# Set-up order of a DLRM tower: look-ups among the first folds, additions after the products, gathers in step with set-up

## Chip, cores and metric

The kernel runs on one core of one Trainium2 chip. The time is device microseconds of the whole program, as the median of its runs. PE is TensorE, DVE VectorE, ACT ScalarE, POOL GpSimd, SP SyncE. All arithmetic is in float32.

## What is computed

26 embedding tables are looked up for 512 rows of ids (EMB 32); a compressed interaction network of two layers without an activation between is summed over the embedding axis, and three dense layers follow:

```python
e  = stack([tbl_f[ids[:, f]] for f in range(26)], axis=1)         # 512 x 26 x 32
x1 = einsum('bik,bjk,hij->bhk', e, e, W1) + b1[None, :, None]      # H = 128
x2 = einsum('bik,bjk,hij->bhk', x1, e, W2) + b2[None, :, None]
z  = concatenate([x1, x2], axis=1).sum(-1)                         # 512 x 256
h  = maximum(concatenate([z, dense_ctx], axis=1) @ W_top1 + b_top1, 0)
h  = maximum(h @ W_top2 + b_top2, 0)
y  = h @ W_top3
```

## The kernel before

The batch is four tiles of 128 rows. Per tile there are four kinds of work.

**Rows.** Ten small tables stay in SBUF (`small`). `one_hot(t)` (L644) makes one-hot matrices of their ids on DVE; `look_up(t, pick)` (L301) multiplies them on PE with the tables, in eight picks that alternate between banks 7 and 6; `pick(t, i)` (L671) masks and sums the result on DVE into `rows`. A look-up waits for the mask of the pick two before it. The other 16 fields come by gathers of POOL, one indirect DMA each, in three parts (`PARTS`: fields 0 to 12, 13 to 22, 23 to 25; of them gathered 5 to 12, 18 to 22 and 23 to 25). In tile 0 the gathers wait for `s_sf`, the count of ACT's set-up copies, by `PACE`; in the later tiles POOL waits for landings at the five places in `PAUSES`.

**Products.** `turn(t, part)` (L692) transposes rows into `prod` on DVE. `take_factor` (ACT, L556) copies a part as factors into bank 6 or 7; `spread` (ACT, L547) writes its block-diagonal form `diag`. `half_a` and `half_b` (DVE, L701, L705) form the products of pairs of fields. `step(t, s)` (L350) then does tile t's product matmuls in four steps of 8 + 8 (L367, L375); ACT's `evict` (L519) copies them to `t0` and `t1`, in tile 0 also the bands, four copies a step, counted by `s_eg`.

**Dense part.** `z2`, `z2_low`, `z1`, `layer1`, `layer2`, `layer3` follow on PE, with ACT's copies of z and the ReLUs between them.

**Set-up**, once: the 35 jobs of `SETUP`. 13 folds (two fields each) and 2 x 5 cross jobs (`ctA`, `ctB`) multiply W1 with W2 on PE (L333, L338); ACT's `take(q)` (L496) copies each. DVE adds the parts up (`low_terms`, `cross_a`, `cross_b`, L729); `s_cross` counts these three groups. Twelve jobs of transposes (v0, v1; L344, L347) bring the sums to where `z2` wants them. The first four, v0's high half, want two groups, its low half all three. `make(q)` (L323) waits until the bank of the job is free (`HOME`, `FREE`). w2t comes in three parts on ACT's queue; the folds 0, 3 and 7 wait for a part each.

The order on each engine is the order of the code. PE runs 10 matmuls without use (`WARM`), then folds and cross jobs with tile 0's look-ups behind the jobs that `BEHIND` names, then 30 more matmuls without use (`FILLS`), partly behind `s_turn`, then tile 0's steps. It then waits for all of ACT's evictions and bands, makes the transposes, and does tile 0's z with tile 1's look-ups at the end of it. DVE does tile 0's picks, additions between the products, `one_hot(1)`, the cross additions, and then tile 1's picks. SP loads idb (ids of the small tables), `small` in two halves, idb's second part, and, when all folds are copied, w1t and the top weights; then idb of tiles 2 and 3.

## Time and profile before

| | us |
|---|---|
| median of 3 runs | 177.43 (177.38 to 177.8) |
| the profiled execution | 179.06 |
| its span, first to last instruction | 177.3 |
| PE busy in the span | 163.7 (92%) |
| DVE, ACT, POOL busy | 112.8, 86.8, 69.0 |

The profile is of one execution. Times in it count from the start of its span. PE's matmuls in float32 stand as two records each in the trace (x16 is eight matmuls), and look-ups, folds and products stand apart by their line.

### The profile page before, as it was taken

What the parts mean: (1) busy time and instruction counts of PE and PEld (TensorE: products, weight loads), DVE (VectorE), ACT (ScalarE), POOL (GpSimd) and SP (SyncE); (2) the same over time, 40 slices, a digit from 0 to 9 for tenths busy, and PEclk for the clock granted to TensorE, in tenths of its full rate; (3) what the DMA queues carried; (4) which work ended last, traced back from release to release, by engine and by line L of the source; (5) the groups of instructions that cost most, each with busy time, mean ns of one, the idle gap of its engine ahead of it and who ended that gap; (6) DMA issues with size and microseconds to landing.
All of it is one profiled execution on the core that took longest, in us unless ns stands there. A gap on an engine that the chain in (4) does not pass through costs nothing.

```text
span 177.3 us, 3417 instructions
## 1 busy us (share of the span) xinstructions
PE 163.7 (92%) x1305; PEld 153.8 (87%) x1305; DVE 112.8 (64%) x343; ACT 86.8 (49%) x232; POOL 69.0 (39%) x72
## 2 busy tenths in 40 slices
PE   6399999999959999962999999999999999999995
PEld 6399899999949987852999999999999999999993
DVE  5824889999980048959754899955589992332000
ACT  0234429938978400593243639544273854553032
POOL 1744666164965644655447454664500000000000
PEclk9969999999996999996699999999999999999999
DMA  5996069000000000400000000000100000000000
GB/s 158 369 413 239 11 176 362 30 15 6 4 7 11 7 7 13 158 9 11 7 15 9 7 11 15 11 6 13 15 0 4 0 0 0 4 0 4 0 0 0
DMA packets 4802, 9.43 MB, mean 53 GB/s; under 512 B 1553, under 2 KB 3089, under 8 KB 4786
## 3 DMA queue, kind: packets, MB, share of 16 engines
q1 hardware_dynamic: 1986, 5.89, 9.3%
q0 software_dynamic: 2048, 1.05, 4.0%
q10 hardware_dynamic: 752, 2.28, 3.8%
q8 instruction: 10, 0.16, 0.4%
q14 instruction: 6, 0.05, 0.1%
HBM read 9.21 MB, written 0.00 MB: 52 GB/s over the span
## 4 chain that ended last, share of the span: by engine, by line
PE 70%; DVE 18%; DMA 4%; ACT 3%; issue 3%; ACTq 0%; DVEq 0%
PE bank L367 13%; PE bank L380 13%; PE bank L317 11%; DVE folded L729 8%; PE bank L375 8%; PE bank L333 6%; PE bank L389 4%; DMA w2t<-in_w2t_dram 4%; PE bank L419 3%; DVE prod L887 3%; DVE prod L872 2%; PE bank L409 2%; PE bank L407 2%; PE bank L344 2%; PE bank L347 2%
## 5 line engine op out<-in xcount | busy, mean ns | idle before, releaser
L287 POOL DMA_INDIRECT rows<-in_tbl_dram,idx x48 | 52.3, 1090 | 43.8 <-DMA rows<-in_tbl_dram,idx 33.7
L367 PE MATMUL bank<-diag,prod 128*128 128x108 f32 x256 | 33.1, 285 | 4.9 <-DVE prod L887 4.9
L367 PEld LDWEIGHTS bank<-diag,prod 128*128 128x128 f32 x256 | 31.9, 200 | 5.6 <-issue 5.3
L682 DVE TENSOR_TENSOR w1p<-bank,chosen 128x320 f32<-128x320 f32 (+2 forms) x32 | 17.0, 531 | 21.0 <-PE bank L317 18.1
L552 ACT ACTIVATE diag<-prod,quad 128x416 f32<-128x416 f32 (+2 forms) x48 | 22.2, 541 | 9.0 <-DVE prod L698 9.0
L380 PEld LDWEIGHTS bank<-t,v 128*128 128x128 f32 x208 | 24.9, 192 | 1.3
L721 DVE COPY t<-bank 13x128 f32<-13x128 f32 (+2 forms) x48 | 12.6, 263 | 20.9 <-PE bank L375 20.4
L528 ACT COPY t<-bank 128x432 f32<-128x432 f32 x32 | 15.0, 522 | 21.6 <-PE bank L367 21.5
L380 PE MATMUL bank<-t,v 128*128 128x128 f32 x208 | 25.1, 275 | 0.0
L317 PE MATMUL bank<-small,idb 128*128 128x256 f32 (+1 forms) x80 | 24.7, 418 | 0.0
L279 POOL DMA_INDIRECT rows<-in_tbl_dram,idx x16 | 15.8, 986 | 13.8 <-ACT folded L501 5.3
L375 PE MATMUL bank<-diag,prod 128*77 128x64 f32 x256 | 20.7, 234 | 0.0
L375 PEld LDWEIGHTS bank<-diag,prod 128*77 128x77 f32 x256 | 20.0, 153 | 0.0
L687 DVE TENSOR_REDUCE rows<-w1p 128x32 f32<-128x320 f32 (+2 forms) x32 | 16.9, 528 | 1.1
L317 PEld LDWEIGHTS bank<-small,idb 128*128 128x128 f32 x80 | 13.4, 190 | 3.1 <-issue 1.0
L537 ACT COPY t<-bank 55x256 f32<-55x256 f32 (+2 forms) x48 | 14.1, 293 | 3.1 <-PE bank L375 2.6
L887 DVE TENSOR_TENSOR prod<-bank,prod 128x364 f32<-128x364 f32 x32 | 14.6, 528 | 0.1
L333 PE MATMUL bank<-w1s,w2t 128*128 128x183 f32 x52 | 11.0, 361 | 2.8 <-DMA w2t<-in_w2t_dram 2.8
L333 PEld LDWEIGHTS bank<-w1s,w2t 128*128 128x128 f32 x52 | 10.1, 221 | 3.6 <-issue 3.0
L501 ACT COPY folded<-bank 128x366 f32<-128x366 f32 x13 | 6.0, 464 | 11.4 <-PE bank L333 9.5
L729 DVE TENSOR_TENSOR folded<-folded,ct 128x52 f32<-128x52 f32 (+13 forms) x51 | 11.2, 294 | 0.1
L872 DVE TENSOR_TENSOR prod<-bank,prod 128x160 f32<-128x160 f32 (+5 forms) x44 | 8.4, 268 | 1.8 <-ACT bank L561 1.8
(71 smaller groups left out, 191.3 us busy)
## 6 DMA issues: line engine op xcount, KB each, us to landing
idb<-in_idt_dram SPq DMA_DIRECT2D x4, 640.0 KB, 4.1
rows<-in_tbl_dram,idx POOLq DMA_INDIRECT x64
wt<-in_W_top_dram SPq DMA_DIRECT2D x2, 512.0 KB
small<-in_small_dram SPq DMA_DIRECT2D x1, 768.0 KB
w2t<-in_w2t_dram ACTq DMA_DIRECT2D x1, 768.0 KB
small<-in_small_dram SPq DMA_DIRECT2D x1, 672.0 KB
w1t<-in_w1t_dram SPq DMA_DIRECT2D x1, 640.0 KB
w1p<-in_w1p_dram ACTq DMA_DIRECT2D x1, 521.0 KB, 4.1
```

Of the source, the lines that this page charges most:

```text
L279: pool.indirect_dma_start(rows[0][:, f, :], None, tables[f], bass.IndirectOffsetOnAxis(ap=idx[:, 0, f:f + 1], axis=0)).then_inc(s_got[0][p ...
L287: pool.indirect_dma_start(rows[t][:, f, :], None, tables[f], bass.IndirectOffsetOnAxis(ap=idx[:, t, f:f + 1], axis=0)).then_inc(s_got[t][p ...
L317: mm = nc.tensor.matmul(ps[:, c], onehot[:, t % 2, e * P:(e + 1) * P], small[:, SPLACE[e]:SPLACE[e + 1]], start=True, stop=True)
L333: mm = nc.tensor.matmul(ps[:, i * PAIRS:(i + 1) * PAIRS], w2t[:, x0 + i, :], w1s[:, 0:PAIRS], start=True, stop=True)
L367: mm = nc.tensor.matmul(m0[:, g % GBANK, :, 0:JW], prod[:, G, 0:P], diag[:, G, :, :], start=True, stop=True)
L375: mm = nc.tensor.matmul(m1[:, g], prod[:, G, P:P + M1], diag[:, G, :, JLOW:], start=True, stop=True)
L380: mm = nc.tensor.matmul(Z2[:, 0:P], v0[:, J2[j], :], t0[:, J2[j], :], start=j == 0, stop=end and j == j1 - 1)
L552: ins = nc.scalar.activation(diag[:, :, r, f0:f1], prod[:, :, col:col + f1 - f0], ACT.Identity, scale=quad[:, r:r + 1])
L682: nc.vector.tensor_tensor(picked[:, 0:width].rearrange("p (f k c) -> p f k c", f=n, c=cs), arrive(i)[:, 0:width].rearrange("p (f k c) -> p ...
L687: nc.vector.tensor_reduce(rows[t][:, SMALL[e0]:SMALL[e0] + n, :], picked[:, 0:width].rearrange("p (f k c) -> p f k c", f=n, c=cs), mybir.A ...
L729: ins = nc.vector.tensor_tensor(dest, dest, term[second], ALU.add)
L887: return eng.tensor_tensor(dst, left, right, ALU.mult)
```

## The change

Constants first. Tile 0's look-ups follow folds 1 to 8 instead of jobs 5 to 13. `WARM` is 22 and `FILLS` is gone. `PACE` has 22 entries, so six gathers of tile 1 also follow ACT's set-up copies, and POOL no longer waits for all landings of tile 0. `HOME` for the transposes uses banks 0 to 4, bank 1 once and bank 5 never.

```diff
-PACE = [0, 0, 0, 0, 1, 4, 6, 8, 9, 10, 12, 13, 14, 15, 16, 17]
+PACE = [0, 0, 0, 0, 0, 1, 2, 3, 3, 4, 5, 6, 7, 8, 9, 10, 12, 13, 14, 15, 17, 18]
-WARM = 10
-FILLS = [16, 8, 6]
+WARM = 22
-HOME = [RING[q % len(RING)] for q in range(DONE["ctB"])] + [0, 1, 2, 0] + [3, 4, 5, 3] + [4, 5, 0, 3]
+HOME = [RING[q % len(RING)] for q in range(DONE["ctB"])] + [0, 1, 2, 3] + [4, 0, 2, 3] + [4, 0, 2, 3]
-BEHIND = {5: 0, 6: 1, 8: 2, 9: 3, 10: 4, 11: 5, 12: 6, 13: 7}
+BEHIND = {1: 0, 2: 1, 3: 2, 4: 3, 5: 4, 6: 5, 7: 6, 8: 7}
```

Queues. w2t's last part goes from ACT's queue to SP's, ahead of idb's second part; w1t, W_top1 and W_top2 wait for tile 0's first, second and third step.

```diff
+            (j0, j1), got = W2PARTS[-1], s_w2[-1]
+            sp.dma_start(w2t[:, j0:j1, :], io["w2t"][:, j0:j1, :]).then_inc(got, 16)
             sp.dma_start(idb[:, 1, :], on_all(io["idt"], 1)).then_inc(s_idb[1], 16)
-            sp.wait_ge(s_sf, FOLDS)
+            sp.wait_ge(s_m0, 1)
             sp.dma_start(w1t[:], io["w1t"]).then_inc(s_w1t, 16)
+            sp.wait_ge(s_m0, 2)
...
+            sp.wait_ge(s_m0, 3)
...
-            for part, (_, f1, _, g0) in enumerate(PARTS):
-                pool.wait_ge(s_got[0][part], 16 * (f1 - g0))
-            for t in range(1, TILES):
+            for t in range(TILES):
                 for part, (_, f1, _, g0) in enumerate(PARTS):
                     for f in range(g0, f1):
+                        if issued < len(PACE) and PACE[issued]:
+                            pool.wait_ge(s_sf, PACE[issued])
+                        issued += 1
...
-                        if (part, f) in PAUSES:
+                        if issued >= len(PACE) and (part, f) in PAUSES:
```

PE. Behind tile 0's steps come two look-ups of tile 1; the transposes wait for three of the four steps' copies, and the other six look-ups stand one by one in the work up to z.

```diff
             for s in range(STEPS):
                 step(0, s)
-            pe.wait_ge(s_e0, STEPS)
-            pe.wait_ge(s_e1, STEPS)
-            pe.wait_ge(s_eg, STEPS)
-            for q in range(DONE["ctB"], DONE["v1"]):
+            look_up(1, 0)
+            look_up(1, 1)
+            pe.wait_ge(s_e0, STEPS - 1)
+            pe.wait_ge(s_e1, STEPS - 1)
+            pe.wait_ge(s_eg, STEPS - 1)
+            for q in range(DONE["ctB"], HIGH):
+                if HOME[q] == 3:
+                    pe.wait_ge(s_e0, STEPS)
+                make(q)
+            for q in range(HIGH, DONE["v1"]):
                 make(q)
             pe.wait_ge(s_sf, HIGH)
             z2(0, HALF)
+            look_up(1, 2)
+            pe.wait_ge(s_eg, STEPS)
             for q in range(DONE["v1"], len(SETUP)):
                 make(q)
+            look_up(1, 3)
             pe.wait_ge(s_sf, DONE["v1"])
             z2_low(0, False)
-            look_up(1, 0)
-            look_up(1, 1)
+            look_up(1, 4)
             pe.wait_ge(s_sf, len(SETUP))
-            for i, (j0, j1) in enumerate(((13, 17), (17, 22), (22, FIELDS))):
+            for i, (j0, j1) in enumerate(((13, 17), (17, 21), (21, FIELDS))):
                 z2(j0, j1, j1 == FIELDS)
-                look_up(1, 2 + 2 * i)
-                look_up(1, 3 + 2 * i)
+                look_up(1, 5 + i)
```

ACT loses tile 0's factor copies, puts the last step's bands behind the copies of the first four transposes, and takes tile 1's factors ahead of z. DVE makes tile 0's factors itself, does products and `one_hot(1)` ahead of all additions, and the z1w addition behind the second pick of tile 1.

```diff
             for q in range(FOLDS + 1):
                 take(q)
-            take_factor(0, 0)
-            for q in range(FOLDS + 1, FOLDS + 5):
+            spread(0, 0)
+            for q in range(FOLDS + 1, DONE["ctB"]):
                 take(q)
-            spread(0, 0)
-            for q in range(FOLDS + 5, DONE["ctB"]):
-                take(q)
-            take_factor(0, 1)
             spread(0, 1)
             spread(0, 2)
             evict(0)
-            for q in range(DONE["ctB"], len(SETUP)):
+            for q in range(DONE["ctB"], HIGH):
+                take(q)
+            put_bands(STEPS - 1)
+            for q in range(HIGH, len(SETUP)):
                 take(q)
...
+                if more:
+                    spread(t + 1, 0)
+                    take_factor(t + 1, 0)
+                    take_factor(t + 1, 1)
+                if more and t:
+                    spread(t + 1, 1)
                 act.wait_ge(s_z2, t + 1)
...
             turn(0, 0)
-            dve.wait_ge(s_sf, FOLDS)
+            first_factors(0)
+            half_a(0)
+            turn(0, 1)
+            first_factors(1)
+            half_b(0)
+            one_hot(1)
+            dve.wait_ge(s_sf, DONE["ctA"])
             low = low_terms(folded)
             add(low, 0, False)
-            half_a(0)
-            turn(0, 1)
             add(low, 1, True)
-            one_hot(1)
-            half_b(0)
-            dve.wait_ge(s_sf, DONE["ctA"])
             cross = cross_a(folded, ct[0])
```

The new function on DVE:

```python
def first_factors(part):
    f0, f1, col, _ = PARTS[part]
    dve.wait_ge(s_turn[part], 1)
    nc.vector.tensor_copy(factors[part][:, :, 0:f1 - f0], prod[:, :, col:col + f1 - f0]).then_inc(s_fac[part], 1)
    if part == 1:
        nc.vector.tensor_copy(prod[:, :, COL_B + HALF:COL_B + HALF + WRAP],
                              prod[:, :, COL_B:COL_B + WRAP]).then_inc(s_dup, 1)
```

In the rows that follow a matmul is named by what it writes and reads: `w1s,w2t` are folds (183 columns) and cross jobs (169), `small,idb` look-ups, `diag,prod` products of the steps, `ident,folded` transposes, `t,v` z2. PE at its start, before:

```order
L299 MATMUL bank<-ident 128x128 x10
L333 MATMUL bank<-w1s,w2t 128x183 x12
L317 MATMUL bank<-small,idb 128x256 x2
L333 MATMUL bank<-w1s,w2t 128x183 x2
L317 MATMUL bank<-small,idb 128x256 x2
L333 MATMUL bank<-w1s,w2t 128x183 x4
L317 MATMUL bank<-small,idb 128x320
```

and after:

```order
L295 MATMUL bank<-ident 128x128 x22
L329 MATMUL bank<-w1s,w2t 128x183 x4
L313 MATMUL bank<-small,idb 128x256 x2
L329 MATMUL bank<-w1s,w2t 128x183 x2
L313 MATMUL bank<-small,idb 128x256 x2
L329 MATMUL bank<-w1s,w2t 128x183 x2
L313 MATMUL bank<-small,idb 128x320
```

The first look-up stood behind six folds (12 matmuls) and now stands behind two. PE around tile 0's last step, before:

```order
L367 MATMUL bank<-diag,prod 128x4x27 x8
L375 MATMUL bank<-diag,prod 77x64 x8
L344 MATMUL bank<-ident,folded 128x128 x13
L347 MATMUL bank<-ident,folded 55x128 x15
L380 MATMUL bank<-t,v 128x128 x13
L344 MATMUL bank<-ident,folded 128x128 x13
L389 MATMUL bank<-t,v 128x128 x8
L317 MATMUL bank<-small,idb 128x256 x4
```

and after:

```order
L363 MATMUL bank<-diag,prod 128x4x27 x8
L371 MATMUL bank<-diag,prod 77x64 x8
L313 MATMUL bank<-small,idb 128x256 x4
L340 MATMUL bank<-ident,folded 128x128 x13
L343 MATMUL bank<-ident,folded 55x128 x15
L376 MATMUL bank<-t,v 128x128 x13
L313 MATMUL bank<-small,idb 128x320
L340 MATMUL bank<-ident,folded 128x128 x13
L313 MATMUL bank<-small,idb 128x256
L385 MATMUL bank<-t,v 128x128 x8
```

The first two look-ups of tile 1 moved ahead of the transposes, and the third and fourth into the work behind them. ACT between the last fold copy and tile 0's first eviction, before:

```order
L504 COPY ct<-bank 128x507
L561 COPY bank<-prod 128x416
L504 COPY ct<-bank 128x507 x3
L504 COPY ct<-bank 128x169
L552 ACTIVATE diag<-prod,quad 128x32x13 x4
L504 COPY ct<-bank 128x507 x4
L504 COPY ct<-bank 128x169
L561 COPY bank<-prod 128x32x10
L563 COPY prod<-prod 128x32x6
L552 ACTIVATE diag<-prod,quad 128x32x10 x4
L552 ACTIVATE diag<-prod,quad 128x32x3 x4
```

and after:

```order
L501 COPY ct<-bank 128x507
L552 ACTIVATE diag<-prod,quad 128x32x13 x4
L501 COPY ct<-bank 128x507 x3
L501 COPY ct<-bank 128x169
L501 COPY ct<-bank 128x507 x4
L501 COPY ct<-bank 128x169
L552 ACTIVATE diag<-prod,quad 128x32x10 x4
L552 ACTIVATE diag<-prod,quad 128x32x3 x4
```

The three factor copies (L561, L563) left ACT here, and spread 0 moved ahead of four of the cross copies.

## Rows read from the trace of the kernel before

**Rows 1.** Windows view: stretch, then busy us of each engine, clock, DMA.
```profile
83.00:177.30 94.30, 92.20 (x794) 86.73 (x794) 54.66 (x143) 42.62 (x118) 24.18 (x26) 0.98 0.04 6
```

**Rows 2.** Timeline of PE: start us, us, instruction, idle before and what ended it.
```profile
1.43 4.55 PE L299 MATMUL bank<-ident 128*128 128x128 f32 x20 [1.43 <-POOL ident L268]
8.78 5.63 PE L333 MATMUL bank<-w1s,w2t 128*128 128x183 f32 x24 [2.80 <-DMA w2t<-in_w2t_dram]
...
31.32 7.09 PE L439 MATMUL bank<-ident 128*128 128x128 f32 x60 [0.27 <-ACT ct L504]
38.25 1.94 PE L367 MATMUL bank<-diag,prod 128*128 128x108 f32 x16
...
52.18 1.77 PE L344 MATMUL bank<-ident,folded 128*128 128x128 f32 x13 [2.16 <-DVE folded L729]
...
71.96 0.38 PE L394 MATMUL bank<-t,z1w 128*128 128x128 f32 x2
...
83.02 3.72 PE L367 MATMUL bank<-diag,prod 128*128 128x108 f32 x16 [4.88 <-DVE prod L887]
```

**Rows 3.** Page, part 2: granted clock in 40 slices of 4.43 us, in tenths.
```profile
PEclk9969999999996999996699999999999999999999
```

**Rows 4.** Timeline of ACT up to tile 0's last eviction.
```profile
28.49 2.31 ACT L552 ACTIVATE diag<-prod,quad 128x416 f32<-128x416 f32 x4
30.68 2.24 ACT L504 COPY ct<-bank 128x507 f32<-128x507 f32 x5
...
33.95 1.95 ACT L552 ACTIVATE diag<-prod,quad 128x320 f32<-128x320 f32 x4
36.78 1.29 ACT L552 ACTIVATE diag<-prod,quad 128x96 f32<-128x96 f32 x4 [0.88 <-DVE prod L698]
...
50.99 0.98 ACT L544 COPY t<-bank 13x128 f32<-13x128 f32 x4
```

**Rows 5.** Timeline of DVE: one-hot, transposes, end of additions, products A of tile 1.
```profile
8.09 0.92 DVE L647 TENSOR_SCALAR idb<-idb 128x1280 int32<-128x1280 int32 x1 [0.63 <-DMA idb<-in_idt_dram]
...
25.49 0.91 DVE L698 STREAM_TRANSPOSE prod<-rows 128x416 f32<-128x416 f32 x1
...
51.94 0.81 DVE L758 TENSOR_TENSOR z1w<-w1t 128x640 f32<-128x640 f32 x1
...
74.65 0.76 DVE L698 STREAM_TRANSPOSE prod<-rows 128x320 f32<-128x320 f32 x1
77.25 2.09 DVE L872 TENSOR_TENSOR prod<-bank,prod 128x160 f32<-128x160 f32 x11 [1.84 <-ACT bank L561]
```

**Rows 6.** Chain of work that ended last, in order of time: start us, us, what.
```profile
14.41 0.86 PE bank L317 x4
...
18.00 0.54 PE bank L317 x2
18.54 0.62 PE bank L333 x4
...
63.42 1.92 PE bank L317 x8
...
86.74 1.59 PE bank L375 x16
...
89.92 1.77 PE bank L367 x16
91.69 1.09 PE bank L375 x16
```

**Rows 7.** DMA view, SP's queue: packets, MB; span's first 7, then 10 us.
```profile
q1 hardware_dynamic: 286, 0.73, 30.3%
...
q1 hardware_dynamic: 427, 1.42, 38.0%
```

**Rows 8.** Windows view at the rise of the clock after 83 us; columns as in rows 1.
```profile
87.50:87.70 0.20, 0.20 (x4) 0.20 (x4) 0.00 (x0) 0.20 (x1) 0.00 (x0) 0.55 0.00 0
```

**Rows 9.** Timeline of POOL: a gather beside DVE's additions.
```profile
44.84 5.24 POOL L287 DMA_INDIRECT rows<-in_tbl_dram,idx  x1 [0.30 <-issue]
```

More of the change, by code:

```diff
@@ L490, in _ @@
             act.dma_start(w1p[:], io["w1p"]).then_inc(s_w1p, 16)
-            for i, (j0, j1) in enumerate(W2PARTS):
+            for i, (j0, j1) in enumerate(W2PARTS[:-1]):
                 act.dma_start(w2t[:, j0:j1, :], io["w2t"][:, j0:j1, :]).then_inc(s_w2[i], 16)
@@ L756, in _ @@
             add(cross, 1, True)
-            dve.wait_ge(s_w1t, 16)
-            nc.vector.tensor_tensor(z1w[:], w1t[:, 0, :, :], w1t[:, 1, :, :], ALU.add).then_inc(s_z1w, 1)
             for i in range(len(PICKS)):
                 pick(1, i)
+                if i == 1:
+                    dve.wait_ge(s_w1t, 16)
+                    nc.vector.tensor_tensor(z1w[:], w1t[:, 0, :, :], w1t[:, 1, :, :], ALU.add).then_inc(s_z1w, 1)
                 if i == 5:
```

44 lines of the change are left out of this document (12 added, 32 removed).

## Prediction

> **What bounds the kernel now.** I read the windows first, then PE's timeline, then the chain of waits. After 83 us PE is busy for 92.2 of 94.3 us [rows 1]: that is tiles 1 to 3, whose code the change leaves alone, so the time is set by when tile 1's first product matmul (L367) starts. It starts at 83.02, after 4.88 us without work [rows 2]. Everything before it is set-up and tile 0. PE's rows show where that time lies: folds from 8.78, additions' matmuls (ct) until 31.05, 30 filler matmuls from 31.32, tile 0's products from 38.25, transposes from 52.18, last look-ups done at 71.96 [rows 2]. The clock row has its low digits in slices 2, 12 and 18 to 19 [rows 3]: after each long idle stretch PE works at half rate, 1.2 GHz, and gets 2.4 GHz back only later.
>
> Tile 0's products waited for DVE's transpose of the last three fields, and for ACT's spread of it, which is in its timeline at 36.78 and lasts 1.29 us [rows 4]: end 38.07, PE 38.25. The transposes at 52.18 are put down to DVE's additions; the code wants only the first two groups of these for them, but it also wants ACT's last band copies, which end at 50.99 + 0.98 = 51.97 [rows 4]. So I take ACT as the releaser there. Tile 1's products waited for DVE's products, which waited 1.84 us for ACT's factor copy (77.25) [rows 5]: ACT had that behind z, a spread and four ReLUs.
>
> **Front of PE.** The first fold waits for w2t and starts at 8.78 as before: nothing ahead of that part moves on its queue. The 22 warm-up matmuls: the ten of before end at 5.98, at half rate (4.55 us for ten) [rows 2]. Twelve more take 12 x 0.24 = 2.8 us at full rate (30 fillers took 7.09) or 5.5 at half; I take full, since the next work, the fold at 8.78, began at a granted clock above the low level: slice 1 still shows 9 [rows 3]. They end near 8.8 and cost nothing, and folds run at full rate, which is what hides them; without it rival 1 prices them.
> Two folds are 4 x 0.31 = 1.24 us (0.62 for a fold of two) [rows 6], to 10.0. Then look-up 0 waits for the first half of small. No row shows its landing: before, it was there by the first look-up, at 14.25. Its queue had moved 0.73 MB at 7.0 us and 1.42 MB at 10.0 [rows 7]. idb's first part is complete at 0.71 MB and landed at about 8.05 (DVE waited for it until 8.09 [rows 5]), 1.1 us after the byte count. The small half is complete at 1.40 MB, so near 9.9 + 1.1 = 11.0. Bounds: 10.0 and 14.1; I take 11.0, the one with a measured lag, so PE waits 1.0.
> In all PE has 13 folds (26 x 0.31 = 8.06) and eight look-ups (2 x 0.86 + 5 x 0.54 + 0.43 = 4.85) [rows 6]: 8.78 + 8.06 + 4.85 + 1.0 = 22.7. The look-ups wait for picks of two before, but a fold stands between each two, so DVE (about 1.0 us for a pick of 320) keeps up. The ct matmuls are 26 of 169 columns for 183: 26 x 0.31 x 169/183 = 7.4, to 30.1. w2t's last part goes to the other queue ahead of idb's second part; by bytes it lands near 15, and fold 7 wants it at 18; idb's second part is wanted at 33.
>
> **Start of tile 0's products.** DVE's picks end near 21.5 instead of 25.5. From there DVE's transpose (0.9), its own factor copies (new on DVE: 416, 320 and 192 elements, some 1.5 us by ACT's price for the same and by DVE's own small copy), products A (4.0), two transposes (1.1) put the start of products B near 29.5 and their end near 33. The price of the copies is an estimate; nothing hangs on it, since ACT comes later. ACT: PE has the first ct job (three matmuls) ready at 23.6, its copy ends at 24.3, spread 0 takes 2.31, nine ct copies 9 x 0.45 = 4.0 (five took 2.24), spread 1 1.95, spread 2 1.29 [rows 4]: 24.3 + 2.3 + 4.0 + 1.95 + 1.3 = 33.9. So the ACT copies and spreads end last, not DVE. Products start at 34.0, not 38.25: **minus 4.2**. Of the 22 gathers that now follow ACT's copies the 16th, tile 0's last, goes out when the tenth fold has been copied (about 21.3) and by 24.8; landing takes 2 to 3.6 us, and DVE wants it at 28.7. POOL's wait for tile 0's landings goes, so tile 1's first six are out by 32. SP's queue now waits for tile 0's first three steps with w1t and the top weights (about 37, 40 and 45); z1 wants them after 65. Behind those waits stands idb's third part, for a one-hot after 76. None of these costs anything.
>
> **Clock.** The fillers are gone, and PE is idle from 30.1 to 34.0. Idle stretches of 2.80, 2.16 and 4.88 us were each followed by half rate [rows 2, 3]. The one of 4.88 is nearest: PE started at 83.02 and had full rate only in the window at 87.5 to 87.7 [rows 8], so 4.65 us at half, which lose **plus 2.3**. Bounds: 1.1 (rate back after 2.2 us) and 2.8. Four steps take 11.8 at full rate (1.77 + 1.09 and a gap each [rows 6]), as 38.25 to 50.03 was; ACT's eviction of a step is as long, and not behind. So products end at 34.0 + 11.8 + 2.3 = 48.1.
>
> **From there to tile 1's look-ups.** Look-ups 0 and 1 of tile 1 (1.92 us [rows 6]) now fill PE while ACT copies the last step: they end at 50.05. Transposes start then, not at 52.18: they need no band of the last step, and DVE's first two groups of additions are done near 44. I add DVE's way to its end: 26.5 us from 25.49 to the z1w addition at 51.94 [rows 5], plus 1.5 for the copies, from 21.5: 49.5. Picks of tile 1 then have 4 us of slack before look-up 2.
> The stretch 52.18 to 71.96 was 19.8 us [rows 2]. Off it go the two look-ups (1.9) and the half rate of slice 12 (digit 6 of a 4.4 us slice: 1.7 lost) [rows 3], since PE has been busy for 16 us; and 0.7 of waits for picks, which now have a product stretch between each two look-ups. Against that the ring for the transposes is five banks and one waits for ACT; I find 3.5 us from the first transpose to z2, as before. 15.5 us, to 65.6, not 71.96: **minus 6.4** for all so far.
>
> **Start of tile 1's products.** Before, 83.02 - 71.96 = 11.1 us. ACT's factor copies now come before z and the ReLUs, so after the last look-up come a pick (1.1), the transpose (0.76 [rows 5]) and then products A, 67.6 instead of 77.25. From there to PE it was 5.8 us; 5.9 now, ACT's spread 2 ending last. PE starts at 73.5: **minus 9.5**.
> In the first step PE then has full rate: before 3.71 + 1.59, at full rate 1.77 + 1.09 [rows 6], 2.4 less. But the look-up behind it needs DVE's next one-hot, which ends 4.6 us after PE's start (two instructions behind the last products B), while step and last layer take 3.4: 0.9 of the 2.4 goes back. **Minus 1.5.**
> Sum: -11.0 us. Against the profiled execution: its span falls from 177.3 to 166.3, its own time from 179.06 to 168.1, with the same 1.8 us around the span. That execution is 1.6 us above the median of the runs, 177.43; I subtract from the median: **166.4 us**.
> **Gathers beside additions.** A gather issued while DVE added folded weights took 5.24 us, 0.94 without the hold, and ended at 50.08, where DVE had a gap [rows 9]. After the change ten gathers of tile 1 are left at 34.7, with three waits for landing of 2.2 among them: 34.7 + 10 x 1.25 + 6.6 = 53.8, and 58 with one such hold; DVE wants the last at 72. The Trainium skill, SBUF — State Buffer, "Who interferes with whom", says that a VectorE instruction with two SBUF inputs, or one in a two-port mode, shuts GpSimd out of a shared port for its whole length. The trace agrees with that. By the page no gather need pass before the additions end at 49.5, and the last would land near 69: still no cost, but 3 us of slack for 14, which is why rival 3 has a chance at all.
>
> **Rivals.**
> 1. Clock low at one more place: at the start if the warm-up's last twelve run at half rate (5.98 + 5.5 = 11.5, and the first look-up starts at 12.7, not 11.0: +1.7), or again before tile 1's products, where PE has gaps of 1.2, 0.2 and 0.8 us within 6 (+1.7). For it: 2.16 us idle was enough once. Against: these gaps are shorter and have work between. 168.1. The Trainium skill, TensorE: Matmul & The Clock Gate, Part 1, says that how many matmuls run slow at the start differs from run to run; no run shown here bears that out, and the three times of before lie within 0.4 us.
> 2. Small arrives late: at 14.1, the far bound. PE waits 4.1 for 1.0 and then has 1.7 of half rate: +4.8, 171.2. Against it: the byte count.
> 3. Slower than before: **gathers held off by DVE**, beside additions and beside the picks of tile 1 too. If tile 1's ten take 4.2 us each, between 1.25 and the 5.54 of the held one [rows 9], the last lands at 34.7 + 42 + 6.6 = 83.3, and PE starts 1.5 later, at 84.8, with half rate as before: 1.8 over 83.02, 179.2. It decides from 4.0 us a gather on. Against: one such gather is in the rows, beside additions alone, and DVE's groups have gaps.
> 4. Better: small there at 10, and the rate back after 2.2 us of products: -1.0 - 1.2, 164.2.
> 5. The change doesn't do what it says at tile 0: DVE is 8 us late with the transpose of the last fields (gathers, or copies of factors far dearer than on ACT), products start at 38 as before and 4.2 us stay out: 170.6.
>
> **How the numbers follow.** Forecast 0.60 (its own range 165 to 168), rival 1 0.16, rival 2 0.05, rival 3 0.04, rival 4 0.10, rival 5 0.03, and 0.02 for no change. Range: to 163.5 below (rival 4, with hardly a loss by the clock) and 169.7 above (both places of rival 1). About 0.3% is what a measurement of this kernel can tell from no change. All but rival 3 and the last case are faster: 0.94, 0.02, 0.04.
>
> **What would show it.** Look-up 0 of tile 0 near 11.0; ct matmuls ending near 30; no PE work from there to 34.0, products released by ACT's spread, clock 0.50 at their start; first transpose near 50; last look-up of tile 1 near 65.6; products A of tile 1 without a wait for ACT; tile 1's products near 73.5 at full rate. It would be wrong if POOL's gathers of tile 1 are still landing after 70, if PE waits in the folds for the second half of small or w2t, or if the clock stays low through tile 0's products.

## The result and the profile after

The kernel after the change takes **167.46 us** (median of four runs: 166.95, 167.01, 167.91, 168.15), the kernel before 177.41 in the same comparison (177.35 to 177.8). The ratio is 0.9437, with a 95% interval of 0.9393 to 0.9482. The forecast was 166.4, with a range of 163.5 to 169.7. Here and below a ratio and its interval leave out executions that lay more than 1.5% above the fastest of their kernel, while a median takes all of them.

| | before | after | difference |
|---|---|---|---|
| median of the runs, us | 177.41 | 167.46 | -9.95 |
| the profiled execution's own time, us | 179.06 | 166.95 | -12.11 |
| its span, us | 177.3 | 165.2 | -12.1 |
| start of tile 1's first product matmul, us | 83.02 | 73.41 | -9.6 |
| from there to the end of the span, us | 94.3 | 91.8 | -2.5 |

The profiled execution of before lay 1.65 above its median, the one of after 0.5 below. That is why the spans differ by 12.1 and the medians by 9.95.

First the page of after: its span and the clock row that answers to [rows 3] (slices of 4.13 us here).

```profile
span 165.2 us, 3343 instructions
...
PEclk9999999969999999789999999999999999999999
```

The clock is low in slice 8 (33 to 37 us, the start of tile 0's products) and in slices 16 and 17 (66 to 74 us). The first was forecast; the second is rival 1's second place.

PE's timeline of after, answering to [rows 2] (start us, us, instruction, idle before and what ended it; windows cut the rows, so a group may be shown in pieces):

```profile
1.43 7.63 PE L295 MATMUL bank<-ident 128*128 128x128 f32 x44 [1.43 <-POOL ident L271]
...
10.82 1.10 PE L313 MATMUL bank<-small,idb 128*128 128x256 f32 x4 [0.52 <-DMA small<-in_small_dram]
...
22.57 7.62 PE L334 MATMUL bank<-w1s,w2t 128*128 128x169 f32 x52
33.83 3.63 PE L363 MATMUL bank<-diag,prod 128*128 128x108 f32 x16 [3.64 <-ACT diag L552]
37.26 1.30 PE L371 MATMUL bank<-diag,prod 128*77 128x64 f32 x16
38.40 1.99 PE L363 MATMUL bank<-diag,prod 128*128 128x108 f32 x16
...
47.15 1.94 PE L313 MATMUL bank<-small,idb 128*128 128x256 f32 x8
48.92 1.58 PE L340 MATMUL bank<-ident,folded 128*128 128x128 f32 x13
...
64.52 0.38 PE L390 MATMUL bank<-t,z1w 128*128 128x128 f32 x2
...
67.62 0.48 PE L403 MATMUL bank<-dctx,wt1c 16*128 16x128 f32 x2 [0.97 <-ACT z L606]
68.03 2.08 PE L405 MATMUL bank<-z,wt 128*128 128x128 f32 x8
...
73.41 2.01 PE L363 MATMUL bank<-diag,prod 128*128 128x108 f32 x16
...
76.96 1.13 PE L313 MATMUL bank<-small,idb 128*128 128x256 f32 x4
77.93 1.93 PE L363 MATMUL bank<-diag,prod 128*128 128x108 f32 x16
```

Nearly every place of the forecast is in these rows. The first look-up starts at 10.82 after 0.52 us of waiting for `small`. The cross matmuls (L334) end at 30.2. PE then has nothing to do until ACT's spread (L552) releases the products at 33.83, and the first eight product matmuls (16 records) take 3.63 us where the next eight take 1.99: that is the half rate. Two look-ups fill the time between the last step and the transposes at 48.92. The last look-up is done where L390 starts, 64.52; L390 is the first matmul of tile 0's z1, and stretches below are counted from it. After that comes what the sum had not got: PE waits 0.97 us for z, and the four matmuls of L405 (8 records) then take 2.08 us. The windows show the clock there (columns as in rows 1):

```profile
73.40:165.20 91.80, 89.74 (x795) 84.43 (x794) 53.27 (x140) 43.24 (x120) 22.85 (x24) 1.00 0.04 6
34.00:35.00 1.00, 1.00 (x6) 1.00 (x6) 1.00 (x4) 0.00 (x0) 0.84 (x1) 0.50 0.00 0
69.00:70.00 1.00, 1.00 (x7) 1.00 (x6) 1.00 (x3) 0.57 (x2) 0.21 (x1) 0.50 0.03 8
```

The column after the five engines is the granted clock: 0.50 (1.2 GHz) at 34 and at 69, 1.00 (2.4 GHz) over the whole rest from 73.4, whose 91.80 us answer to the 94.30 of [rows 1].

ACT's timeline of after around tile 0's products and around z, answering to [rows 4]:

```profile
30.61 3.12 ACT L552 ACTIVATE diag<-prod,quad 128x320 f32<-128x320 f32 x8
...
67.21 0.36 ACT L606 ACTIVATE z<-bank,b2x 128x128 f32<-128x128 f32 x1
...
67.61 1.96 ACT L552 ACTIVATE diag<-prod,quad 128x320 f32<-128x320 f32 x4
70.57 1.54 ACT L569 ACTIVATE h<-bank,vec 128x128 f32<-128x128 f32 x4 [1.00 <-PE bank L408]
72.02 1.29 ACT L552 ACTIVATE diag<-prod,quad 128x96 f32<-128x96 f32 x4
```

The last two spreads of tile 0 end at 33.73, 0.1 before PE starts. At 67 us the price of the new order shows: z stands behind two factor copies that wait for DVE's transpose, so z comes at 67.57; PE idles, slows, and ACT's ReLUs (L569) wait 1.00 us for it, which pushes the spread of tile 1's last fields to 72.02.

DVE's additions, transposes and products A, answering to [rows 5], and POOL's gathers beside the additions and behind them, answering to [rows 9]:

```profile
28.72 0.33 DVE L692 STREAM_TRANSPOSE prod<-rows 128x96 f32<-128x96 f32 x1
...
38.89 11.32 DVE L732 TENSOR_TENSOR folded<-folded,ct 128x65 f32<-128x65 f32 x51
...
66.41 2.05 DVE L877 TENSOR_TENSOR prod<-bank,prod 128x160 f32<-128x160 f32 x11
```
```profile
37.17 0.95 POOL L283 DMA_INDIRECT rows<-in_tbl_dram,idx  x1 [0.31 <-issue]
42.92 2.98 POOL L283 DMA_INDIRECT rows<-in_tbl_dram,idx  x1 [4.81 <-DMA rows<-in_tbl_dram,idx]
46.21 2.03 POOL L283 DMA_INDIRECT rows<-in_tbl_dram,idx  x1 [0.30 <-issue]
48.54 2.49 POOL L283 DMA_INDIRECT rows<-in_tbl_dram,idx  x1 [0.30 <-issue]
...
60.60 0.95 POOL L283 DMA_INDIRECT rows<-in_tbl_dram,idx  x1 [2.26 <-DMA rows<-in_tbl_dram,idx]
```

Additions end at 50.2. They come in two parts: 44 short ones of 0.10 us each from 34.70 to 38.96, then the 51 in the row above, of 0.22 us each. Two gathers issued beside the short ones took 0.95 us each (35.91 and 37.17), as those behind the additions do; the three issued beside the longer ones took 2.0 to 3.0. Tile 1's last goes out at 57.40, and the one behind it waits until 60.60 for tile 1's to land. DVE wants them at 70.4, so 10 us are to spare.

### The profile page after: what moved, and what is told of

Same layout as the page of the kernel before. It is cut to its first block, busy times and chain, and to the rows that moved or that the text cites. A ratio compares the mean times of both kernels' runs of the same rounds, so it can differ in the third digit from the quotient of the medians.

```text
span 165.2 us, 3343 instructions
## 1 busy us (share of the span) xinstructions
PE 156.6 (95%) x1269; PEld 147.8 (89%) x1269; DVE 114.1 (69%) x346; ACT 86.1 (52%) x229; POOL 68.0 (41%) x72
## 3 DMA queue, kind: packets, MB, share of 16 engines
q1 hardware_dynamic: 2130, 6.68, 11.5%
q0 software_dynamic: 2048, 1.05, 4.2%
## 4 chain that ended last, share of the span: by engine, by line
PE 88%; DMA 5%; ACT 3%; DVE 1%; SPq 0%; issue 0%; DVEq 0%
PE bank L363 19%; PE bank L376 14%; PE bank L313 13%; PE bank L371 11%; DMA small<-in_small_dram 5%; PE bank L385 5%; PE bank L334 4%; PE bank L415 4%; PE bank L329 4%; PE bank L405 3%; PE bank L408 3%; PE bank L403 2%; ACT diag L552 2%; PE bank L340 2%; PE bank L392 2%; PE bank L423 1%
## 5 line engine op out<-in xcount | busy, mean ns | idle before, releaser
L283 POOL DMA_INDIRECT rows<-in_tbl_dram,idx x64 | 67.1, 1049 | 46.3 <-DMA rows<-in_tbl_dram,idx 28.2
L552 ACT ACTIVATE diag<-prod,quad 128x416 f32<-128x416 f32 (+2 forms) x48 | 22.0, 539 | 12.1 <-DVE prod L692 12.1
L371 PE MATMUL bank<-diag,prod 128*77 128x64 f32 x256 | 20.2, 230 | 0.0
L371 PEld LDWEIGHTS bank<-diag,prod 128*77 128x77 f32 x256 | 19.5, 149 | 0.0
L313 PEld LDWEIGHTS bank<-small,idb 128*128 128x128 f32 x80 | 13.4, 191 | 2.4 <-issue 1.2
L732 DVE TENSOR_TENSOR folded<-folded,ct 128x52 f32<-128x52 f32 (+13 forms) x51 | 11.2, 301 | 0.1
L329 PE MATMUL bank<-w1s,w2t 128*128 128x183 f32 x52 | 9.5, 318 | 0.0
L329 PEld LDWEIGHTS bank<-w1s,w2t 128*128 128x128 f32 x52 | 8.6, 190 | 0.9
L295 PE MATMUL bank<-ident 128*128 128x128 f32 x44 | 7.6, 356 | 1.4 <-POOL ident L271 1.4
L295 PEld LDWEIGHTS bank<-ident 128*128 128x128 f32 x44 | 7.4, 269 | 1.4 <-POOL ident L271 1.4
```

Source lines behind the costliest of these rows:

```text
L283: pool.indirect_dma_start(rows[t][:, f, :], None, tables[f], bass.IndirectOffsetOnAxis(ap=idx[:, t, f:f + 1], axis=0)).then_inc(s_got[t][p ...
L295: nc.tensor.matmul(bank[7][:, 0:P], ident[:], ident[:], start=True, stop=True)
L313: mm = nc.tensor.matmul(ps[:, c], onehot[:, t % 2, e * P:(e + 1) * P], small[:, SPLACE[e]:SPLACE[e + 1]], start=True, stop=True)
L329: mm = nc.tensor.matmul(ps[:, i * PAIRS:(i + 1) * PAIRS], w2t[:, x0 + i, :], w1s[:, 0:PAIRS], start=True, stop=True)
L371: mm = nc.tensor.matmul(m1[:, g], prod[:, G, P:P + M1], diag[:, G, :, JLOW:], start=True, stop=True)
L552: ins = nc.scalar.activation(diag[:, :, r, f0:f1], prod[:, :, col:col + f1 - f0], ACT.Identity, scale=quad[:, r:r + 1])
```

## Experiments

Each run is told with what was expected of it; where A and B stand, A is my account of the change as the prediction and the trace of after gave it, B the rival for that run. The kernel before ran beside each group, on the same chip: c1_after, e5_best, e6_addfirst and e7_looklast together (before 177.77); e1 to e4 together (before 179.46, from 177.27 to 182.04); e8 to e11 together (before 179.44, from 178.1 to 181.24). In the last two groups the kernels' traces have idle stretches of DVE and ACT that the others lack, 1 to 5.7 us at a time, in the folds, look-ups and cross jobs and again near 91 and 121 us. So times of those groups are compared within a group only, and I lean on stretches within their traces. A line of ACT from e4_best and one of DVE from e10_latelook show such stretches:

```profile
34.02 3.42 ACT L504 COPY ct<-bank 128x507 f32<-128x507 f32 x8 [3.72 <-remote]
```
```profile
23.38 0.49 DVE L676 TENSOR_TENSOR w1p<-bank,chosen 128x320 f32<-128x320 f32 x1 [5.74 <-remote]
```

The releaser is put down as "remote": the profile names nothing of this core's program that ended these waits. Some of the stretches go by another name: in e8_fill DVE's pick at 18.92 comes after 1.84 us without work, put down to a look-up of PE, which had ended at 17.91.

### The changed kernel again

c1_after is the changed kernel itself, as the control of its group.

> The changed kernel again, beside the others of this call. If the idle time of DVE and ACT between 16 and 34 us that the first four kernels show (2 to 4 us at a time, released by nothing in the profile) came with that chip, this run is at 167.5 +- 0.7 on another chip, or, on the same one, near 173 to 175 beside the kernel before at 179. If it came with those kernels' edits, this run is at 167.5 on the same chip.

Measured: 166.85 us (166.69 to 166.96 in five runs, 167.84 in the profiled one); ratio 0.9398 (0.9365 to 0.9431). That is the first of the two expected cases: no such idle stretch, on another chip. e5_best and e4_best below are the same kernel, with the stretches in one and not in the other, so they did not come with the edits. Its profiled execution shows where the upper of its two levels comes from. PE's timeline at tile 0's products and at z1:

```profile
33.65 3.72 PE L363 MATMUL bank<-diag,prod 128*128 128x108 f32 x16 [3.65 <-ACT diag L552]
37.16 2.26 PE L371 MATMUL bank<-diag,prod 128*77 128x64 f32 x16
39.22 2.16 PE L363 MATMUL bank<-diag,prod 128*128 128x108 f32 x16
...
65.52 0.38 PE L390 MATMUL bank<-t,z1w 128*128 128x128 f32 x2
```

The idle stretch ahead is the same as in after (3.65 and 3.64 us), yet the half rate goes on through L371 (2.26 for 1.30) and into the second step. Products start 0.18 earlier, and L390 comes 1.00 later. The two executions' own times differ by 0.9 (167.84 and 166.95), as do the two levels of the four runs above. So in these two traces **1 us of this kernel's time depends on when the clock comes back**: the first step lost 1.7 us to it in after and the first two lost 2.8 in c1_after. For the other runs that is a likely cause and no more, as there is no trace of them; the mean granted clocks on record go with it for the 167.91 (0.968, with 0.969 for the 167.84 here) and not for the 168.15 (0.979, as for the 166.95). The Trainium skill, TensorE: Matmul & The Clock Gate, Part 1, says that how many matmuls run slow at a kernel's start differs from run to run. The traces agree: the 22 warm-up matmuls take from 6.72 us (e1_fill) to 8.12 (e3_zmid) in the thirteen that have them. Of this the start of tile 0's products keeps little (33.65 to 33.94 in after, c1_after, e5_best and e7_looklast).

### Work for PE ahead of tile 0's products (e1_fill, e8_fill)

```diff
+            pe.wait_ge(s_sf, FREE[DONE["ctB"]])
+            for _ in range(14):
+                nc.tensor.matmul(bank[0][:, 0:P], ident[:], ident[:], start=True, stop=True)
             for s in range(STEPS):
                 step(0, s)
```

> The changed kernel with 14 matmuls without use put between the cross jobs and tile 0's steps (3.3 us of work in PE's 3.64 us of idle time). Theory A (half rate after the idle stretch costs the first step 1.8 us, and PE's chain up to tile 1's products passes this on): first step's 16 records near 1.8 us instead of 3.63, 165.6 to 166.2 for 167.46. Rival B (what follows waits for ACT or DVE, so PE's loss is hidden): first step faster, tile 1's products still at 73.4, 167.2 to 167.6. Rival C (fillers are late themselves and push the steps): slower by up to 0.5.

> 14 fillers between the cross jobs and tile 0's steps, alone, as in the first of these runs, whose chip held DVE and ACT up. In the changed kernel the first step runs at half rate for 1.8 to 3.1 us of loss (two traces), and the stretch up to tile 1's products is PE's. Theory A: 165.0 to 165.6, for 166.85 to 167.46 of the changed kernel, tile 1's products near 71.6 to 72.3. Rival B (the gain ends in the wait for z): 166.3 or more. The kernel with both edits had 164.97; the rest to that is what z's order is worth.

Measured: e1_fill 173.95 (171.02 to 177.45), without a usable ratio; e8_fill 172.39, ratio 0.9583 (0.9519 to 0.9646). The times say little, since the idle stretches above put tile 0's products at 39.5 and 40.4. PE's timeline of e8_fill shows the mechanism:

```profile
35.81 3.31 PE L432 MATMUL bank<-ident 128*128 128x128 f32 x28
40.42 2.01 PE L363 MATMUL bank<-diag,prod 128*128 128x108 f32 x16 [1.29 <-issue]
...
72.58 0.48 PE L403 MATMUL bank<-dctx,wt1c 16*128 16x128 f32 x2 [0.96 <-ACT z L609]
```

With 1.29 us idle ahead of them instead of 3.6, the first eight product matmuls take 2.01 us (2.01 in e1_fill too, behind 0.94), so the half rate there is due to the idle stretch that the change opened. The wait for z (0.96) stays, and so does the fall of the clock behind it: from L390 to tile 1's products it is 8.81 and 8.82 us, as in the changed kernel.

### z between the two factor copies (e3_zmid), and both together (e4_best, e5_best)

```diff
                 if more:
                     spread(t + 1, 0)
                     take_factor(t + 1, 0)
-                    take_factor(t + 1, 1)
                 if more and t:
+                    take_factor(t + 1, 1)
                     spread(t + 1, 1)
...
                 nc.scalar.copy(z[0][:], Z1[:, 0:P]).then_inc(s_z1s, 1)
+                if t == 0:
+                    take_factor(1, 1)
```

> The changed kernel with z's two copies on ACT ahead of tile 1's second factor copy instead of behind it. Theory A (PE's wait of 0.97 us for z and the half rate from 68.05 to 71.5 behind it delay the ReLUs, and with them the spread that tile 1's products wait for): no wait at z, clock stays high, products near 72.2, 166.2 to 166.6. Rival B (products wait for DVE's transpose of the last fields at 70.7 and its spread in any case): 167.2 to 167.6.

> Both: 14 fillers ahead of tile 0's steps, and z ahead of the second factor copy. Theory A: the two gains add, 164.3 to 165.0. Rival B: one of them is hidden behind DVE's chain, 165.6 to 166.4.

> 14 fillers ahead of tile 0's steps and z ahead of tile 1's second factor copy, as before, now beside the changed kernel itself. Theory A (half rate in the first step, and the wait for z with the half rate behind it, are on the path): 2.5 to 3.0 us below the changed kernel. Rival B (one of the two is hidden by DVE's chain): 1.2 to 1.8 below. Rival C (hidden both): within 0.5.

Measured: e3_zmid 174.08, ratio 0.973 (0.9678 to 0.9782); e4_best 172.67, ratio 0.9646 (0.9579 to 0.9713). **e5_best**, the same kernel as e4_best beside the control: **164.97** (164.78 to 165.07), ratio 0.9284 (0.9255 to 0.9313), 1.9 us below the control and faster than both kernels of this case. PE's timeline of e5_best:

```profile
33.94 2.01 PE L363 MATMUL bank<-diag,prod 128*128 128x108 f32 x16 [0.53 <-issue]
...
62.99 0.38 PE L390 MATMUL bank<-t,z1w 128*128 128x128 f32 x2
64.20 1.35 PE L403 MATMUL bank<-dctx,wt1c 16*128 16x128 f32 x8
65.48 1.16 PE L405 MATMUL bank<-z,wt 128*128 128x128 f32 x8
...
70.64 2.00 PE L363 MATMUL bank<-diag,prod 128*128 128x108 f32 x16 [0.65 <-DVE prod L897]
...
75.00 1.13 PE L313 MATMUL bank<-small,idb 128*128 128x256 f32 x4 [0.74 <-DVE idb L648]
75.97 1.93 PE L363 MATMUL bank<-diag,prod 128*128 128x108 f32 x16
```

L390 comes 1.53 us earlier than in after: the filler's part, which is the 1.65 us that the first step had lost (4.57 us to the second step in after, 2.92 between later ones), less the 0.11 by which the products start later. L403 runs without a break, and L405 takes 1.16 us for 2.08. In e3_zmid the same edit alone takes the wait and the fall away, as A had it; the products then wait for DVE's last transpose and ACT's spread of it, as B had it. From L390 to tile 1's products it is 7.65 us instead of 8.89, but 0.8 of that is given back at once, because PE now waits 0.74 us for the one-hot of tile 2. In sum -1.53 - 1.24 + 0.8 = -1.97, beside -1.88 measured between the medians. The expectation named 2.5 to 3.0 under A and 1.2 to 1.8 under B; it was neither, for A left out the new wait. What each edit is worth alone wasn't measured in a run of this group; the parts are read from traces.

e6_addfirst, told below, settles what in this was the wait and what the clock. Its order of z is that of the changed kernel, and PE waits 0.96 us for z there too, but L405 then takes 1.16 us and the clock doesn't fall:

```profile
68.48 0.39 PE L390 MATMUL bank<-t,z1w 128*128 128x128 f32 x2
...
71.58 0.48 PE L403 MATMUL bank<-dctx,wt1c 16*128 16x128 f32 x2 [0.96 <-ACT z L606]
72.00 1.16 PE L405 MATMUL bank<-z,wt 128*128 128x128 f32 x8
```

From L390 (68.48) to the products (76.13) it is 7.65 us, the same as with the new order. So **the wait for z costs nothing by itself**, since what ends last is DVE's last transpose and ACT's spread of it (to 76.03); the 1.24 us are the clock alone, and e3_zmid and e5_best save them by taking that idle stretch away. Seven traces have this wait, of 0.96 to 1.05 us, and the granted clock fell to 0.50 behind it in all of them but e6_addfirst; in the six traces of this change's variants without it, it didn't fall there. With the one-hot counted in, the stretch from L390 to the second product step is:

| kernels | L390 to tile 1's products | to its second step |
|---|---|---|
| after, c1_after: wait for z, clock falls | 8.89, 8.81 | 13.41, 13.26 |
| e7_looklast, e1_fill, e8_fill, e10_latelook: the same | 8.90, 8.81, 8.82, 8.89 | 13.35, 13.26, 13.55, 13.42 |
| e6_addfirst: wait for z, clock stays | 7.65 | 12.97 |
| e3_zmid, e4_best, e5_best: no wait | 7.65, 7.64, 7.65 | 13.05, 12.99, 12.98 |
| e11_best_oh: no wait, one-hot of tile 2 earlier | 7.65 | 12.18 |

The fall of the clock is worth 1.2 us in the second column and only 0.4 in the third.

### Tile 2's one-hot earlier (e11_best_oh)

The kernel of e5_best, with the one-hot among the picks of tile 1:

```diff
+                if i == 3:
+                    one_hot(2)
...
-                if more:
+                if more and t > 1:
                     one_hot(t + 1)
```

> The version with fillers and z ahead, and tile 2's one-hot moved from behind tile 1's products B to behind the fourth pick of tile 1, where DVE waits 1.8 us for PE. In the version without it PE waited 0.76 us and then some for that one-hot behind the first step of tile 1. Theory A: that wait goes, 164.0 to 164.3 for 164.97. Rival B (DVE is late with the fifth pick, and tile 1's products move by as much): 164.9 to 165.5.

Measured: 172.28 (six executions, of which the ratio counts two, 169.35 and 170.48), ratio 0.9479 (0.939 to 0.9569), beside 0.9583 (0.9519 to 0.9646) for e8_fill in the same group. The intervals overlap, so the gain in time isn't established. PE's timeline shows the step, though:

```profile
76.94 2.01 PE L363 MATMUL bank<-diag,prod 128*128 128x108 f32 x16 [0.65 <-DVE prod L899]
...
80.50 1.13 PE L313 MATMUL bank<-small,idb 128*128 128x256 f32 x4
81.47 1.93 PE L363 MATMUL bank<-diag,prod 128*128 128x108 f32 x16
```

The look-up has no wait left, the second step follows 4.53 us after the first (5.33 in e5_best), and the picks lose nothing by it: from L385 to L390 it is 7.2 us in both. The 0.8 us are there in the trace; that they reach the end of a run without the idle stretches wasn't measured.

### Tile 1's factors back behind z (e2_factail, e9_factail)

For tile 0's layers the factor copies and spreads of ACT go back to where the kernel before had them:

```diff
-                if more:
+                if more and t:
...
                 if more:
-                    spread(t + 1, 2 if t else 1)
+                    spread(t + 1, 2 if t else 0)
                 relu1(t)
                 if t == 0:
-                    spread(1, 2)
+                    take_factor(1, 0)
+                    take_factor(1, 1)
+                    spread(1, 1)
                 relu2(t)
+                if t == 0:
+                    spread(1, 2)
```

> The changed kernel with ACT's tile 1 order of before: spread 0 and the factor copies behind z and the ReLUs. Theory A (the order brought the cut from 11.1 to 9.0 us between last look-up and tile 1's products): products A of tile 1 wait for ACT again, tile 1's products near 75.5, 169.5 to 170. Rival B (DVE's picks, moved up by one look-up each, brought it): products near 73.4 to 74, 167.5 to 168.

> ACT's tile 1 order of before (spread 0 and factor copies behind z and the ReLUs), alone, again. Theory A: products A of tile 1 wait 1.8 us or more for ACT, tile 1's products near 75.5, 169 to 170. Rival B (moving the picks up did it): 167 to 168.

Measured: 178.52, ratio 0.9941 (0.9889 to 0.9992), and 179.89, ratio 0.9996 (0.9946 to 1.0045). Over the executions that the ratios count the medians are 178.05 and 179.41, which is 6.4 over e1_fill (171.61, of two such only) and 7.0 over e8_fill (172.39) of their groups; about 1.5 of each is the filler's, as e5_best shows. DVE's timeline of e9_factail, and PE's:

```profile
78.76 2.08 DVE L880 TENSOR_TENSOR prod<-bank,prod 128x160 f32<-128x160 f32 x11 [3.42 <-ACT bank L561]
```
```profile
73.31 0.38 PE L390 MATMUL bank<-t,z1w 128*128 128x128 f32 x2
...
84.53 3.72 PE L363 MATMUL bank<-diag,prod 128*128 128x108 f32 x16 [4.87 <-DVE prod L895]
```

From L390 to the products it is 11.2 us again, as the 11.1 of before (71.96 to 83.02), against 8.9 after the change and 7.65 where the clock holds. DVE waits 3.42 us for ACT's factor copy; in [rows 5] it was 1.84. The 4.87 us idle bring the half rate back to the first step as well (3.72), and in e2_factail the second product step comes 18.5 us behind L390 (71.02 and 89.50), against 13.4 in after and 17.8 in before (71.96, and 89.75 in its timeline). That is 5.1 us for this one edit (5.4 in e9_factail, 73.31 and 92.14), the largest part that a run here showed, and it fits the 6.4 and 7.0 less the filler's part. The place was as expected and the loss larger: DVE's transpose now comes 1.3 us behind L390's start instead of 2.7, so it waits longer for the same z, spread and ReLUs of ACT.

### Additions ahead of tile 0's products (e6_addfirst)

```diff
             turn(0, 0)
+            dve.wait_ge(s_sf, FOLDS)
+            low = low_terms(folded)
+            add(low, 0, False)
             first_factors(0)
             half_a(0)
             turn(0, 1)
+            add(low, 1, True)
             first_factors(1)
-            half_b(0)
             one_hot(1)
+            half_b(0)
             dve.wait_ge(s_sf, DONE["ctA"])
```

> The changed kernel with DVE's order of before: the first additions ahead of products A, the second and tile 1's one-hot ahead of products B (ACT's factor copies stay off). Theory A (tile 0's products start when ACT has spread the last three fields, and DVE had only some 2 us to spare there): the last transpose moves from 28.7 to near 34.3, its spread ends at 36 instead of 33.7, products B at 36.5: 2.2 to 3.0 us above the changed kernel. Rival B (ACT's chain hides it): within 0.7 of it.

Measured: 169.92 (169.63 to 170.51), ratio 0.9568 (0.9529 to 0.9607), 3.1 over the control, where A had 2.2 to 3.0. PE's timeline and ACT's:

```profile
36.45 3.72 PE L363 MATMUL bank<-diag,prod 128*128 128x108 f32 x16 [6.28 <-DVE prod L893]
```
```profile
35.06 1.30 ACT L552 ACTIVATE diag<-prod,quad 128x96 f32<-128x96 f32 x4 [2.07 <-DVE prod L692]
```

The products start 2.8 us later than in c1_after (36.45 and 33.65), and the releaser is put down as DVE. What ends last is ACT's spread, at 36.36, which has waited 2.07 us for DVE: its last transpose (34.69 us here, 28.72 in after) now stands behind the first additions and the one-hot. The run moves both of these at once. L390 comes 2.96 later, and the spans differ by 2.7. So the order of DVE's work is part of the gain at this place: without it the products would start 1.8 us before those of [rows 2], not 4.4. The products here have half rate for about as long as in c1_after (36.45 to 42.02 for the first step, 5.57 in both).

### Tile 1's look-ups back behind z2 (e7_looklast)

```diff
                 step(0, s)
-            look_up(1, 0)
-            look_up(1, 1)
             pe.wait_ge(s_e0, STEPS - 1)
-            pe.wait_ge(s_e1, STEPS - 1)
-            pe.wait_ge(s_eg, STEPS - 1)
+            pe.wait_ge(s_e1, STEPS)
+            pe.wait_ge(s_eg, STEPS)
...
             z2(0, HALF)
-            look_up(1, 2)
+            look_up(1, 0)
...
-            look_up(1, 3)
+            look_up(1, 1)
             pe.wait_ge(s_sf, DONE["v1"])
             z2_low(0, False)
+            look_up(1, 2)
+            look_up(1, 3)
             look_up(1, 4)
```

On ACT the last step's bands go back ahead of the copies of the transposes, since the transposes now wait for them:

```diff
             evict(0)
+            put_bands(STEPS - 1)
             for q in range(DONE["ctB"], HIGH):
                 take(q)
-            put_bands(STEPS - 1)
```

> The changed kernel with tile 0's transposes waiting for ACT's last bands again and no look-up of tile 1 ahead of them (look-ups 0 and 1 one place later, 2 to 4 behind z2_low). Theory A (PE waits some 2.2 us for ACT there, and the look-ups filled that): 1.8 to 2.4 above the changed kernel. Rival B (the picks of tile 1 then pile up behind one another on DVE as well): 3 or more above.

Measured: 170.2 (169.67 to 170.68), ratio 0.9579 (0.9537 to 0.962), 3.35 over the control: above what A gave, in B's range. PE's timeline:

```profile
49.53 1.61 PE L340 MATMUL bank<-ident,folded 128*128 128x128 f32 x13 [2.16 <-issue]
```

PE stands idle for 2.16 us ahead of the transposes, as before the change, with ACT still copying the last step's bands until 49.32 (the releaser is put down as "issue"). The transposes start 0.6 us later than in after, at equal end of the products. From there to L390 (67.30) it is 17.8 us, where after has 15.6: 1.8 for the two look-ups that now stand here, and 0.4 more. Together 2.8 us, as the spans of this trace and after's differ by 2.7. That is A's account. B's pile-up of picks can hold no more than the 0.4: the three look-ups that now stand in a row take 2.03 us (60.75 to 62.78) for 0.54 each. The rest up to 3.35 lies within what the runs of one kernel differ by (the four runs of e7_looklast are two near 169.7 and two near 170.65). So the two look-ups cost about nothing where the change put them, in a stretch in which PE had waited anyway.

### Tile 0's look-ups late (e10_latelook)

```diff
-BEHIND = {1: 0, 2: 1, 3: 2, 4: 3, 5: 4, 6: 5, 7: 6, 8: 7}
+BEHIND = {5: 0, 6: 1, 8: 2, 9: 3, 10: 4, 11: 5, 12: 6, 13: 7}
```

> Tile 0's look-ups behind jobs 5 to 13 as before, all else as in the changed kernel: the edit that the change is named after, undone. DVE's picks end 3 to 4 us later (near 25), its last transpose of tile 0 near 32.5 for 28.7, the spread of it near 34.2 for 33.7, additions end near 54 for 50.1. Theory A (DVE had 3 us to spare against ACT, and 5 before tile 1's third pick): only 0.3 to 1.2 above the changed kernel, 167.3 to 168.4. Rival B (the 4 us go through to the end): 170 to 171.

Measured: 175.85, ratio 0.9774 (0.9675 to 0.9873). The three executions that the ratio counts have a median of 175.53, 3.1 over e8_fill of its group, of which about 1.5 is the filler's; that fits neither A nor B. Its trace has DVE's idle stretch of 5.74 us shown above within the picks of tile 0, and one of 3.87 on ACT. Its products wait 4.06 us for DVE and start at 42.14, but what the later look-ups cost can't be parted from these stretches. So what tile 0's early look-ups, the first item of the change, are worth stays open. From L390 to the products it is 8.9 us, as in after.

Three parts, each undone alone, are thus worth 5.1 us (ACT's order for tile 1), 2.8 (tile 1's first look-ups) and 2.7 (DVE's order) of the 12.1 between the spans; they can overlap, so their sum means little. The pace of the gathers, the moved loads of SP, the banks of the transposes, the number of warm-up matmuls and the factor copies moved off ACT in tile 0 were not varied in any run.

## Why the prediction was right, step by step

| step, us | forecast | measured in after |
|---|---|---|
| wait for the first half of `small` | 1.0 | 0.52 |
| cross matmuls start / end | 22.7 / 30.1 | 22.6 / 30.2 |
| tile 0's products start | 34.0 | 33.83 |
| lost to the clock in tile 0's steps | 2.3 | 1.7 |
| products end | 48.1 | 47.3 |
| transposes start | 50.05 | 48.92 |
| additions end | 49.5 | 50.2 |
| last look-up of tile 1 done | 65.6 | 64.5 |
| products A of tile 1 | 67.6 | 66.4 |
| from the last look-up to tile 1's products | 7.9 | 8.9 |
| tile 1's products start | 73.5 | 73.41 |
| behind that | -1.5 | -2.5 |

**The front** held closely. Twelve more warm-up matmuls ended at 9.06, near the 8.8 of full rate, and the fold at 8.90 was 0.12 late. (That the first ten ran at half rate is read from their 4.55 us; the windows view has a granted clock of 1.00 over them, 1.43 to 6.00 in before, so there the column and the durations don't agree.) The landing of `small`, worked out from a byte count and one measured lag, was right to 0.3 us. The three factor copies on DVE took 0.59 + 0.49 + 0.49 = 1.57 (estimated 1.5), and ACT set the start of the products, as the sum had it.

**The clock at tile 0's products**: right in kind, and in size within what the executions differ by, 1.7 in one and 2.8 in the other. Over all eight traces with half rate there the loss is 1.6 to 3.0; the lower bound of 1.1 had no row behind it, and no run came near it. e1_fill, e5_best and e8_fill showed the cause.

**Tile 1's products at 73.5 was right by luck: two errors cancel.** Everything up to the last look-up came 1.1 us earlier than summed, in small parts (0.17 at the start, 0.6 of clock, 0.1 in the steps at full rate, the look-ups' 1.77 for 1.92); the stretch from the transposes to the last look-up was right (15.5, measured 15.6). The 7.9 us behind it should have been 7.65 by the work alone and became 8.9, because rival 1's second place came true: the clock fell again. The prediction had set three gaps of 1.2, 0.2 and 0.8 us against this, as shorter than the 2.16 that had once been enough. One gap of about 1 us was enough in after, in c1_after and in four more traces, and was not in e6_addfirst.

**The term -1.5 was mis-sized**: it measured -2.5, of which 2.2 lie between tile 1's first two product steps (6.73 us before, 4.52 after). The step at fault is "0.9 of the 2.4 goes back" to the wait for tile 2's one-hot. The one-hot ended at 76.46 and the look-up started at 76.96 without a wait, for the slow clock had delayed PE against DVE. In e5_best, where PE isn't delayed, the wait came at 0.74, so the reading of the order was right and its condition was not. The term has a slip in it too: a one-hot that ends at 4.6 us behind 3.4 us of work makes a wait of 1.2, not 0.9, and would have given -1.2 and 166.7.

**The last step** was the weakest: -11.0 was summed against the profiled execution and then subtracted from the median. On spans the change gave -12.1, on medians -9.95. Against the profiled execution's own time the same sum gave 168.1, 1.1 above the 166.95 of after's; against the median it gave 166.4, 1.1 below the 167.46. Before's profiled execution stood 1.65 above its median, and which part of its rows held that surplus, no row tells.

**The rivals.** Rival 1: its first place, half rate up to 11.5 at the start, did not come; its second did, at +1.24 for the start of tile 1's products and +0.4 for the end. Rival 2 fell with the landing at 10.8. Rival 3 fell: gathers beside additions took 0.95 to 2.98 us against the 4.0 from which it decides, and tile 1's were landed by 60.6, near the 58 of the sum. The Trainium skill, SBUF — State Buffer, "Who interferes with whom", says that a VectorE instruction with two SBUF inputs contends with a GpSimd instruction that reads SBUF, that the shared ports are an exclusive lock, and that the order of issue decides who waits. That is a rule for one instruction at a time, which the prediction stretched over the whole run of additions. The trace agrees that gathers beside the longer additions are slowed, but two passed beside the short ones at their usual 0.95, and two of the three others were done by 48.24, before the additions ended. Of rival 4's early clock about half came in after (1.7 lost, between 2.3 and 1.1) and nothing in c1_after, and of its early `small` half did. Rival 5 fell with products at 33.83.

## What to carry to other kernels

When work is moved ahead of an idle stretch, ask what the fast engine does in the stretch that opens: here 14 filler matmuls and one copy moved behind z gave 1.9 us more. Neither took work away; by the traces it is 2.8 us of clock, less 0.8 for a wait that then showed. Price a wait by what ends last behind it, since the wait for z cost nothing until the clock fell with it. And where the profiled execution stands off its kernel's median by nearly a per cent, a difference of spans can't be carried over to the median closer than that.

## What was new about the hardware

After an idle stretch of the same length (3.64 and 3.65 us) the granted clock came back about 1 us later in one execution than in the other. An idle stretch of only 0.96 to 1.05 us, behind three matmuls that read 16 rows, was followed by a granted clock of 0.50 in six of seven traces: at once in after, only at 70 to 71 us in c1_after, where the wait had ended at 68.61, and not at all in e6_addfirst. What decides between them stays open. The idle stretches put down to "remote" on DVE and ACT (most of them 1 to 5.7 us, in two of the three groups, with before's medians 179.4 in them for 177.8) occurred in no trace of before, of after, or of the third group; their cause is open too.
